# Transformer blocks on one core: the order of SyncE's queue in the block loop, the place of two turned halves, of small buffers and of the last signs

## The chip, the core and the metric

The kernel runs on one core of a Trainium2 chip. Its engines are TensorE (PE, with PEld for its weight loads), VectorE (DVE), ScalarE (ACT), GpSimd (POOL) and SyncE (SP), which here issues DMAs only. Each runs its own stream of instructions, and they order one another by semaphores that the program writes out by hand. The metric is the device time in microseconds. Three runs of the kernel before gave 2302.49, 2304.49 and 2305.18 us.

## The reference

```python
# x: 64 samples x 64 rows x 512; two layers, each x = x + ffn(cond(x))
def _L0_cond_ref(x, subjects, weights):
    return jnp.einsum('bct,bcd->bdt', x, weights[subjects])
def _L0_ffn_ref(x, w_gate_up, w_proj):
    gu = jnp.einsum('bsd,hd->bsh', x, ternary_quant(w_gate_up))
    gate, up = jnp.split(gu, 2, axis=-1)
    h = jax.nn.silu(gate) * up
    return jnp.einsum('bsh,dh->bsd', rms_norm(h), ternary_quant(w_proj))
def _L1_cond_ref(x, W, A, Bm, scalings, adapter_idx):
    H = jnp.einsum('btd,od->bto', x, W)
    xa = jnp.einsum('btd,brd->btr', x, A[adapter_idx])
    delta = jnp.einsum('btr,bor->bto', xa, Bm[adapter_idx])
    return H + delta * scalings[adapter_idx][:, None, None]
def _L1_ffn_ref(hidden_states, router_w, router_b, expert_w, expert_b):
    logits = (h @ router_w.T + router_b).reshape(T, O, E)      # O = 512, E = 8
    w, sel = jax.lax.top_k(jax.nn.softmax(logits, axis=-1), 2)
    w = w / jnp.sum(w, axis=-1, keepdims=True)
    c = jnp.zeros((T, E)).at[t_idx, sel].add(w)                # summed over O
    expert_out = jnp.einsum('th,eoh->teo', h, expert_w) + expert_b[None, :, :]
    return jnp.einsum('te,teo->to', c, expert_out)
```

## The kernel before

The 4096 rows are worked on in two big parts. The **first part** goes by blocks of 512 rows, 8 of them (`NBLK`), numbered 0 to 7. For each block PE mixes the rows with the sample's own 64x64 matrix (`mix`), then runs over 16 chunks of the hidden width (`gu`: 16 matmuls of gate and up; `proj`: 8 matmuls of the down projection of the chunk before), each value kept as a high and a low part, so that two or three matmuls make one product. In between, PE works on the block before: `adapt` (the low-rank product, behind chunk 11), `linear` (behind chunks 12 and 14). Blocks 0 and 1 are interleaved with the quantisation of the weights; blocks 2 to 6 are a hardware loop, and block 7 is written out.

For `adapt` and `linear` the second layer's input must stand with its features on the partitions. The block's result x1 is stored to DRAM by ScalarE (`store_x1`, behind chunk 0 of the next block), and SP fetches it back in 16 transfers in an order by lanes of 32 (`rows_for_turning`, line 505, transfer at line 511) into `rows_by_lane`. DVE turns it in squares of 32 (`turned`, lines 1276 to 1285) in two halves: two transposes into `cols`, ScalarE's high copy `x1t_hi` (line 832), and DVE's low part `x1t_lo` (line 1284). The first half waits for all 16 transfers (line 1279). The halves stand in DVE's stream and in ScalarE's between the chunks, so what a half waits for, the products, low parts (`hid_lo`, line 1232) and sums of the chunks behind it wait for too.

In each of four trips of SP's loop (`with sp.Fori(4, NBLK) as i`, line 519; trip i runs while block i-1 is computed, that is blocks 3 to 6) SP works off this list in order: it waits until block i-1 is mixed; loads `x_mix` for block i (1 MB); gathers eight 64x64 matrices into `mixw`; then makes the differences of the router's weights, seven times over: load a piece (line 529), wait for GpSimd's subtraction (`differences`, lines 704 to 708; line 708 is the subtraction), store it (line 531), wait for the store; and last the rows for turning of block i-2. GpSimd also makes the inverse root of the block's mean square (`power`, line 702), ahead of the differences in its stream. Block 2 has no differences: SP issues its loads and rows ahead of the loop (lines 513 to 518).

The **second part** goes by tiles of 128 rows, 32 of them (`NT`). The router stage fills 7 banks per tile, ScalarE copies them out, makes signs of them (`sign`, `place`) and DVE finds the two largest of eight (`tournament`), joins the placed signs into codes (`join`) and, between tiles, decodes codes and sums choices of earlier tiles (`decode`, `total`). The expert stage then fills 8 banks per tile: ScalarE seeds a bank with the bias (`seed_expert`, line 1098) once DVE has added the same bank of the tile before (`expert`, line 1557), and PE adds 12 matmuls to it (lines 1824 to 1828). At the change from one stage to the other, the last tile's tournament (`last_router`) lies among the experts of tile 1 on DVE; its signs and places lie on ScalarE behind seed 4 of the pass over tile 1, ahead of seeds 5 to 7, which are those of tile 2's banks; and its join stands ahead of tile 2 on DVE. SP stores the joined codes and only then goes on with the loads for tile 4 and 5. ScalarE's weights of tile 4 (`weigh`, lines 1037 and 1038) follow behind the pass over tile 1.

The buffers in SBUF are laid out by the order of the calls of `sb`: a stack that is closed gives its bytes to what is allocated next, and the program's semaphores keep the users apart.

Of the kernel before, what the change touches and what calls it, by code (L numbers as in the profile page):

```python
# [20 lines left out]
F32 = mybir.dt.float32  # L21
F32R = mybir.dt.float32r
BF16 = mybir.dt.bfloat16
I32 = mybir.dt.int32
# [5 lines left out]
P = 128  # L30
D = 512
DC = D // P
NB_SAMPLES = 64
# [9 lines left out]
E = 8  # L43
# [121 lines left out]
def build(nc, x, idx7, idx6, cond_w, w_ffn, WcT, AT, Bt, scal, rwT, rb, ewT, eb, out):  # L165
# [8 lines left out]
    with root:  # L174
        def sb(name, shape, dt, ctx=root):
            return ctx.enter_context(nc.sbuf_tensor(name, shape, dt))
# [6 lines left out]


        ident = sb("ident", [P, P], F32)


        pa = ExitStack()
# [16 lines left out]
        cols = sb("cols", [P, 2, BLK], F32, turning)  # L205
        turning.close()
        hid1 = sb("hid1", [P, RING, BLK], F32, pa)
        group_mean = sb("group_mean", [P, P], BF16, pa)
        py = ExitStack()
        y1_hi = sb("y1_hi", [P, DC, BLK], F32R, py)  # L210
        y1_lo = sb("y1_lo", [P, DC, BLK], F32R, py)
# [11 lines left out]
        x_res = sb("x_res", [P, SUB, D], F32, pa)  # L223
        sq = sb("sq", [P, BLK], F32, pa)
        sumsq = sb("sumsq", [P, BLK], F32, pa)
        ones_col = sb("ones_col", [P, 1], F32, pa)
        var = sb("var", [P, SUB], F32, pa)
        inv = sb("inv", [P, SUB], F32, pa)
        minus_half = sb("minus_half", [P, SUB], F32, pa)
        subject_i = sb("subject_i", [1, NB_SAMPLES], I32, pa)  # L230
        idx_i = sb("idx_i", [P, NB_SAMPLES], I32, pa)
        adapter_i = sb("adapter_i", [P, 1], I32, pa)
        adapter_f = sb("adapter_f", [P, 1], F32, pa)
        scal_sb = sb("scal_sb", [P, 1], F32, pa)
        lmask = sb("lmask", [P, NB_SAMPLES], F32, pa)

        pq = ExitStack()
        q_raw = sb("q_raw", [P, 3, UW], F32, pq)
# [34 lines left out]
        p4.close()  # L273
        bias_sb = sb("bias_sb", [P, E, D], F32, p2)
        wts = sb("wts", [P, 2, 2, D], F32, p2)
        step_col = sb("step_col", [P, 4], F32, p2)

        lead_in = sb("lead_in", [P, 2, D], F32, p2)
        code_in = sb("code_in", [P, 2, 2, D], BF16, p2)
        half_in = sb("half_in", [P, 4, D], U16, p2)  # L280
        digits = sb("digits", [P, 2, D], F32, p2)
        c_ring = sb("c_ring", [P, 4, E], F32, p2)
        p3 = ExitStack()
        acc = sb("acc", [P, 2, D], F32, p3)
        xin = sb("xin", [P, 2, D], F32, p3)
# [148 lines left out]
        def one(ap, i):  # L434

            if isinstance(i, int):
                return ap[i]
            names = " ".join("abcdef"[:len(ap.shape) - 1])
            return ap[bass.ds(i, 1)].rearrange(f"z {names} -> (z a) {names[2:]}"
                                               .replace("(z a)", "(z a)"))  # L440
# [3 lines left out]
        def _(sp):  # L444
            def gather_mix(i, w, done, samples=range(SPB)):
                for q in samples:
                    v = sp.value_load(subject_i[0:1, bass.ds(i * SPB + q, 1)], min_val=0, max_val=E - 1)
                    r = (q % 2) * C
                    sp.dma_start(w[r:r + C, q // 2, r:r + C],
                                 cond_w[bass.ds(v * C, C), :]).then_inc(done, 16)  # L450
# [54 lines left out]
            def rows_for_turning(l):  # L505

                sp.wait_ge(x1_stored, 16 * (l + 1) if isinstance(l, int) else sp.snap(l * 16 + 16))
                src = one(X1L, l) if isinstance(l, int) else X1L[bass.ds(l, 1)].rearrange("z a p c b j -> (z a) p c b j")
                for a in range(P // TOK):
                    for c in range(DC):  # L510
                        sp.dma_start(rows_by_lane[a * TOK:(a + 1) * TOK, c, :, :], src[a, :, c]).then_inc(rows_back, 16)  # L511
# [7 lines left out]
            with sp.Fori(4, NBLK) as i:  # L519

                mixed = sp.snap(use(i - 1, "mix1")[0] + 1)
                sp.wait_ge(drained, mixed)
                sp.dma_start(x_mix[:, :, :], one(XB, i)).then_inc(xmix_in, 16)
                gather_mix(i, mixw, mixw_in)
                piece = one(RWC, i - 4)
                sp.dma_start(diff_base[:, :], piece[0]).then_inc(diff_in, 16)
                to = one(DFC, i - 4)
                for e in range(EP):
                    sp.dma_start(diff_work[:, :], piece[e + 1]).then_inc(diff_in, 16)
                    sp.wait_ge(diff_done, sp.snap(i * EP + (e + 1 - 4 * EP)))  # L530
                    sp.dma_start(to[e], diff_work[:, :]).then_inc(diff_out, 16)
                    sp.wait_ge(diff_out, sp.snap(i * (16 * EP) + 16 * (e + 1 - 4 * EP)))
                sp.wait_ge(x1t_ready, sp.snap(i * 2 - 6))
                rows_for_turning(i - 2)


            def send_h(l, u):
# [185 lines left out]
        def _(act):  # L723
# [204 lines left out]
            def block(i):  # L928
                mix(i)
                for j in range(HC):  # L930
                    silu(i, j)
                    if j == 0:
                        store_x1(i - 1)
                    hidden(i, j)
                    if j == 2:
                        next_rows(i - 1)
                    if j in (9, 10):
                        turned(i - 1, j - 9)
                    if j == 11:
                        adapt(i - 1)  # L940
                    if j == 12 and not isinstance(i, int):
                        store_h(i - 1, 0)
                    if j == HC - 1 and isinstance(i, int):
                        copy_h(i - 1, 0)
                    if j == 14 and not isinstance(i, int):
                        store_h(i - 1, 1)
# [155 lines left out]
            def pair(m):  # L1102

                for u in range(2):
                    if not isinstance(m, int):
                        weigh(m * 2 + (u + 2), u, m + 1)
                    for e in range(E):
                        seed_expert(m * 2 + u, e)
                        if isinstance(m, int) and u == 1 and e == 4:
                            sign(NT - 1, 1, L[:, 0, EP - 1, :], (NT + 1) * KT)  # L1110
                            place(NT - 1)
                    store(m * 2 + u, u)
                    load_h(m * 2 + (u + 2), u)
# [11 lines left out]
        def _(dve):  # L1125
# [229 lines left out]
            def block(i):  # L1355
                mix(i)
                finish(i - 1)
                for j in range(HC):
                    hidden(i, j)
                    if j in (9, 10):  # L1360
                        turned(i - 1, j - 9)
                    if j == 11:
                        adapt(i - 1)
                    if j == (HC - 1 if isinstance(i, int) else 12):
                        split_h(i - 1, 0)
                    if j == 14 and not isinstance(i, int):
                        split_h(i - 1, 1)
# [190 lines left out]
                                               c_ring[:, k, e:e + 1], (xin if e == 0 else acc)[:, u, :],  # L1558
                                               ALU.mult, ALU.add).then_inc(exp_step, 1)

            def tile(n, k, pair):


                for e in range(E):
                    expert(n, e, k, pair)
                    if not isinstance(n, int) or n + 2 < NT:
                        if e == 0:
                            decode(n + 2, (k + 2) % 4)
                        total(n + 2, e, (k + 2) % 4)
# [9 lines left out]
            for e in range(E):  # L1579
                expert(1, e, 1, 0)  # L1580
                if e == 2:
                    last_router()
            join(NT - 1)
            for n in range(2, 4):
                tile(n, n, n // 2)
            with dve.Fori(1, NT // 4 - 1) as m:
                for k in range(4):
                    tile(m * 4 + k, k, m * 2 + k // 2)
# [300 lines left out]
```

## Time and profile before

| | us |
|---|---|
| median of 3 runs | 2304.49 (2302.49 to 2305.18) |
| the profiled execution | 2306.22 |
| its span | 2304.5 |
| PE busy | 2207.9 |
| DVE busy | 1625.1 |
| ScalarE busy | 1053.1 |
| GpSimd busy | 59.3 |

The span is the time from the first to the last instruction of the profiled execution. A busy time counts the engine's own instructions, not waits and not the issue of DMAs. Times of rows below are microseconds from the span's start. On the span lie the quantisation with blocks 0 and 1 (to 231), blocks 2 to 7 (block 2 from 231.06 to 340.19, blocks 3 to 6 to 858.27), the router stage (to about 1600) and the expert stage.

### The profile page before, as it was taken

To read this page: it belongs to the slowest core of one execution; us is meant where nothing else is said; L and a number is where in the kernel's file an instruction comes from. 1 tells how busy PE (TensorE), PEld (TensorE's weight loads), DVE (VectorE), ACT (ScalarE), POOL (GpSimd) and SP (SyncE) were. 2 spreads that over 40 slices of the span, in tenths; PEclk is the share of its full clock that TensorE was granted. 3 is DMA by queue.
4 is the path that set the end of the run, shared out by engine and by line. 5 is a ranking of instruction groups with operands and counts; after the bars stand their busy time and mean duration, and the time that the engine had idled before them with its cause. 6 is when DMAs were issued, how large, how long until landed. Compare 5 with 4: busy or idle time off the path is not lost.

```text
span 2304.5 us, 28740 instructions
## 1 busy us (share of the span) xinstructions
PE 2207.9 (96%) x9817; PEld 1814.9 (79%) x9817; DVE 1625.1 (71%) x2119; ACT 1053.1 (46%) x1493; POOL 59.3 (3%) x55
## 2 busy tenths in 40 slices
PE   7999999696969889999999999999999999999999
PEld 5777888585858678788888888888788888888887
DVE  8985444343433234568999999999898888888883
ACT  7754333232322223367877878778332222222221
POOL 0000001010010100200000000000000000000000
PEclk9999999898989989999999999999999999999999
DMA  6314213231322312532121212116322222222220
GB/s 206 106 41 140 76 37 116 46 116 46 116 64 76 100 40 55 187 110 87 69 77 68 82 68 82 68 68 241 110 96 82 77 96 82 78 96 77 83 82 23
DMA packets 157908, 205.66 MB, mean 89 GB/s; under 512 B 63330, under 2 KB 96674, under 8 KB 155682
## 3 DMA queue, kind: packets, MB, share of 16 engines
q1 hardware_dynamic: 114578, 149.95, 19.6%
q10 hardware_dynamic: 43152, 55.06, 7.3%
q8 instruction: 22, 0.36, 0.1%
q14 instruction: 28, 0.23, 0.0%
q0 software_dynamic: 128, 0.07, 0.0%
HBM read 136.35 MB, written 68.68 MB: 89 GB/s over the span
## 4 chain that ended last, share of the span: by engine, by line
PE 76%; issue 14%; DVE 3%; POOL 2%; ACT 1%; SPq 1%; DMA 1%; POOLq 0%; ACTq 0%; DVEq 0%
PE slot L1650 10%; PE ex_bank L1825 9%; PE ex_bank L1827 9%; PE ex_bank L1826 9%; PE high_bank L1792 5%; PE high_bank L1794 5%; PE high_bank L1796 5%; PE pj L1663 5%; PE low_bank L1792 4%; PE low_bank L1796 4%; PE low_bank L1794 4%; PE slot L1712 3%; POOL diff_work L708 2%; PE slot L1619 1%; SPq L511 1%
## 5 line engine op out<-in xcount | busy, mean ns | idle before, releaser
L1650 PE MATMUL slot<-y_hi,wgu 128*128 128x512 f32 x1024 | 402.0, 393 | 1.1 <-DVE q_scale L1168 0.5
L1650 PE MATMUL slot<-y_lo,wgu 128*128 128x512 f32 x1024 | 399.4, 390 | 0.0
L1825 PE MATMUL ex_bank<-ew_hi,hb 128*128 128x512 f32 x992 | 387.3, 390 | 3.5 <-ACT ex_bank L1098 3.5
L1826 PE MATMUL ex_bank<-ew_hi,hb 128*128 128x512 f32 x992 | 386.8, 390 | 0.0
L1827 PE MATMUL ex_bank<-ew_lo,hb 128*128 128x512 f32 x992 | 386.8, 390 | 0.0
L1098 ACT ACTIVATE ex_bank<-eb_sb 128x512 f32<-128x512 f32 x248 | 149.1, 602 | 456.5 <-DVE acc L1557 395.4
L1507 DVE SCALAR_TENSOR_TENSOR lead_in<-code_in,wts 128x1024 bf16<-128x1024 bf16 x256 | 311.8, 1218 | 1.8 <-DVE code_in L1434 0.4
L1663 PE MATMUL pj<-wpj,hid_hi 128*128 128x512 f32 x484 | 194.7, 402 | 72.5 <-DVE hid_lo L1232 72.5
L1650 PEld LDWEIGHTS slot<-y_hi,wgu 128*128 128x128 f32 x1024 | 192.3, 188 | 44.6 <-DVE q_scale L1168 2.8
L1650 PEld LDWEIGHTS slot<-y_lo,wgu 128*128 128x128 f32 x1024 | 192.4, 188 | 39.7
L1825 PEld LDWEIGHTS ex_bank<-ew_hi,hb 128*128 128x128 f32 x992 | 186.7, 188 | 42.6 <-ACT ex_bank L1098 3.9
L1826 PEld LDWEIGHTS ex_bank<-ew_hi,hb 128*128 128x128 f32 x992 | 186.7, 188 | 38.6
L1827 PEld LDWEIGHTS ex_bank<-ew_lo,hb 128*128 128x128 f32 x992 | 186.6, 188 | 38.8
L1210 DVE TENSOR_TENSOR hid<-gate,slot 128x512 f32<-128x512 f32 x112 | 76.9, 687 | 198.7 <-ACT gate L778 197.9
L778 ACT ACTIVATE gate<-slot 128x512 f32<-128x512 f32 x128 | 76.3, 596 | 284.5 <-PE slot L1650 245.4
L1792 PE MATMUL high_bank<-rw_hi,hb 128*128 128x512 f32 x512 | 199.5, 390 | 0.0
L1794 PE MATMUL high_bank<-rw_hi,hb 128*128 128x512 f32 x512 | 199.4, 390 | 0.0
L1796 PE MATMUL high_bank<-rw_lo,hb 128*128 128x512 f32 x512 | 199.4, 389 | 0.0
L1663 PE MATMUL pj<-wpj,hid_lo 128*128 128x512 f32 x484 | 192.5, 398 | 0.0
L1557 DVE SCALAR_TENSOR_TENSOR acc<-ex_bank,c_ring,acc 128x512 f32<-128x512 f32 x193 | 144.6, 749 | 67.9 <-PE ex_bank L1827 64.8
L1663 PEld LDWEIGHTS pj<-wpj,hid_hi 128*128 128x128 f32 x484 | 93.0, 192 | 93.8 <-DVE hid_lo L1232 74.2
L1792 PE MATMUL low_bank<-rw_hi,hb 128*128 128x512 f32 x384 | 149.6, 390 | 0.0
(169 smaller groups left out, 3560.6 us busy)
## 6 DMA issues: line engine op xcount, KB each, us to landing
hb<-h_scratch SPq DMA_DIRECT2D x34, 512.0 KB, 3.5
code_scratch<-half_code SPq DMA_DIRECT2D x32, 512.0 KB, 2.6
half_in<-code_scratch SPq DMA_DIRECT2D x32, 512.0 KB, 3.3
hb<-h_scratch ACTq DMA_DIRECT2D x30, 512.0 KB, 3.6
h_scratch<-ht ACTq DMA_DIRECT2D x48, 256.0 KB, 2.9
q_raw<-in_w_ffn SPq DMA_DIRECT2D x21, 512.0 KB, 3.4
x_scratch<-x_res ACTq DMA_DIRECT2D x8, 1024.0 KB, 4.4
lead_scratch<-lead SPq DMA_DIRECT2D x32, 256.0 KB, 2.0
```

The lines of the kernel that those rows point to most:

```text
L1098: nc.scalar.activation(ex[e][:, :], eb_sb[:, e, :], ACT.Copy).then_inc(ex_seeded, 1)
L1210: nc.vector.tensor_tensor(hid[:, j % 2, :], gate[:, g, :], slot[s % 2][:, 1, :], ALU.mult).then_inc(drained, 1)
L1507: nc.vector.scalar_tensor_tensor(lead_in[:, k % 2, :].bitcast(BF16).rearrange("p (a n) -> p a n", a=2), code_in[:, k % 2, :, :], float(2 * ...
L1557: nc.vector.scalar_tensor_tensor((res if e == E - 1 and not first else acc)[:, u, :], ex[e][:, :], c_ring[:, k, e:e + 1], (xin if e == 0 e ...
L1650: last = mm(slot[s % 2][:, g, :], wgu[:, c, r * P:(r + 1) * P], y[:, c, :], start=(c == 0 and v == 0), stop=(c == DC - 1 and v == 1))
L1663: last = mm(pj[k][:, :], h[:, k * P:(k + 1) * P], wpj[:, w, :], start=(j == 0 and v == 0), stop=(j == HC - 1 and v == 1))
L1792: mm(plane[k][:, :], hb[:, u, c, 0, :], rw_hi[:, k, c, :], start=False, stop=False, skip_group_check=True)
L1794: mm(plane[k][:, :], hb[:, u, c, 1, :], rw_hi[:, k, c, :], start=False, stop=False, skip_group_check=True)
L1796: last = mm(plane[k][:, :], hb[:, u, c, 0, :], rw_lo[:, k, c, :], start=False, stop=True, skip_group_check=True)
L1825: mm(ex[e][:, :], hb[:, u, c, 0, :], ew_hi[:, e, c, :], start=False, stop=False, skip_group_check=True)
L1826: mm(ex[e][:, :], hb[:, u, c, 1, :], ew_hi[:, e, c, :], start=False, stop=False, skip_group_check=True)
L1827: last = mm(ex[e][:, :], hb[:, u, c, 0, :], ew_lo[:, e, c, :], start=False, stop=(c == DC - 1), skip_group_check=True)
```

## The change

Five edits:

- In SP's loop the rows for turning, with their two waits, go ahead of the differences, and the load of `x_mix` goes behind them, to the end of the trip.
- The two turned halves go one chunk forward, behind chunks 8 and 9 instead of 9 and 10, on ScalarE and on DVE.
- Thirteen small buffers are allocated at the front of SBUF, behind `ident`; everything else shifts.
- ScalarE's last sign and place go behind the last seed of that pass (`e == EP`, seven) instead of behind the fifth.
- DVE's last join goes from in front of tile 2 to behind its expert 4.

```diff
@@ -183,6 +183,24 @@
         ident = sb("ident", [P, P], F32)
+        early_small = ExitStack()
+        group_mean = sb("group_mean", [P, P], BF16, early_small)
+        ones_col = sb("ones_col", [P, 1], F32, early_small)
...
+        scal_sb = sb("scal_sb", [P, 1], F32, early_small)
+        lmask = sb("lmask", [P, NB_SAMPLES], F32, early_small)
+        early_small.close()
+        late_small = ExitStack()
+        step_col = sb("step_col", [P, 4], F32, late_small)
+        c_ring = sb("c_ring", [P, 4, E], F32, late_small)
+        late_small.close()
+        small_end = sb("small_end", [P, 320], F32)
...
@@ -520,8 +525,9 @@
                 mixed = sp.snap(use(i - 1, "mix1")[0] + 1)
                 sp.wait_ge(drained, mixed)
-                sp.dma_start(x_mix[:, :, :], one(XB, i)).then_inc(xmix_in, 16)
                 gather_mix(i, mixw, mixw_in)
+                sp.wait_ge(x1t_ready, sp.snap(i * 2 - 6))
+                rows_for_turning(i - 2)
                 piece = one(RWC, i - 4)
                 sp.dma_start(diff_base[:, :], piece[0]).then_inc(diff_in, 16)
                 to = one(DFC, i - 4)
@@ -530,8 +536,7 @@
                     sp.wait_ge(diff_done, sp.snap(i * EP + (e + 1 - 4 * EP)))
                     sp.dma_start(to[e], diff_work[:, :]).then_inc(diff_out, 16)
                     sp.wait_ge(diff_out, sp.snap(i * (16 * EP) + 16 * (e + 1 - 4 * EP)))
-                sp.wait_ge(x1t_ready, sp.snap(i * 2 - 6))
-                rows_for_turning(i - 2)
+                sp.dma_start(x_mix[:, :, :], one(XB, i)).then_inc(xmix_in, 16)
@@ -934,8 +939,8 @@
-                    if j in (9, 10):
-                        turned(i - 1, j - 9)
+                    if j in (8, 9):
+                        turned(i - 1, j - 8)
@@ -1106,7 +1111,7 @@
                         seed_expert(m * 2 + u, e)
-                        if isinstance(m, int) and u == 1 and e == 4:
+                        if isinstance(m, int) and u == 1 and e == EP:
                             sign(NT - 1, 1, L[:, 0, EP - 1, :], (NT + 1) * KT)
                             place(NT - 1)
@@ -1357,8 +1362,8 @@
-                    if j in (9, 10):
-                        turned(i - 1, j - 9)
+                    if j in (8, 9):
+                        turned(i - 1, j - 8)
@@ -1558,11 +1563,13 @@
-            def tile(n, k, pair):
+            def tile(n, k, pair, between=None):
                 for e in range(E):
                     expert(n, e, k, pair)
+                    if e == 4 and between is not None:
+                        between()
@@ -1580,9 +1587,8 @@
-            join(NT - 1)
-            for n in range(2, 4):
-                tile(n, n, n // 2)
+            tile(2, 2, 1, lambda: join(NT - 1))
+            tile(3, 3, 1)
```

## Rows read from the trace of the kernel before

**Rows 1.** The page, part 1: busy us, share of span, instructions.

```profile
PE 2207.9 (96%) x9817; PEld 1814.9 (79%) x9817; DVE 1625.1 (71%) x2119; ACT 1053.1 (46%) x1493; POOL 59.3 (3%) x55
```

**Rows 2.** Windows, PE alone: stretch, length, busy (matmuls), granted clock, DMA share, GB/s.

```profile
231.06:340.19 109.13, 108.70 (x499) 1.00 0.20 55
340.19:858.27 518.08, 444.06 (x1987) 0.92 0.27 80
```

**Rows 3.** Waits of PE: whom it waited for, us in total, times, longest.

```profile
PE pj L1663 <- DVE hid_lo L1232: 72.5, 4, 19.3
...
PE ex_bank L1825 <- ACT ex_bank L1098: 3.5, 1, 3.5
```

**Rows 4.** Timeline, DVE, block 4: start, us, line, operation [idle before <- releaser].

```profile
507.85 1.50 DVE L1232 TENSOR_TENSOR hid_lo<-hid,hid_hi 128x512 fp32r<-128x512 f32 x1 [0.70 <-ACT hid_hi L789]
...
549.66 1.30 DVE L1281 STREAM_TRANSPOSE cols<-rows_by_lane 128x512 f32<-128x512 f32 x2 [18.76 <-DMA rows_by_lane<-x_scratch]
```

**Rows 5.** Timeline, SP's DMA queue, block 3.

```profile
346.26 0.42 SPq L523 DMA_DIRECT2D x_mix<-in_x  x1
347.55 10.53 SPq L449 DMA_DIRECT2D mixw<-in_cond_w  x8
358.26 0.44 SPq L526 DMA_DIRECT2D diff_base<-in_rwT  x1
...
411.54 8.29 SPq L511 DMA_DIRECT2D rows_by_lane<-x_scratch  x16
```

**Rows 6.** Timeline, SP's DMA queue, block 2.

```profile
238.15 10.47 SPq L449 DMA_DIRECT2D mixw<-in_cond_w  x8
248.74 12.05 SPq L511 DMA_DIRECT2D rows_by_lane<-x_scratch  x16
```

**Rows 7.** Chain that ended last, block 2: start, us, what.

```profile
279.12 3.63 PE slot L1650 x16
282.75 1.81 PE pj L1663 x8
...
301.31 3.06 PE slot L1701 x12
```

**Rows 8.** Timeline, DVE, block 2.

```profile
291.46 1.30 DVE L1281 STREAM_TRANSPOSE cols<-rows_by_lane 128x512 f32<-128x512 f32 x2
...
296.40 0.69 DVE L1232 TENSOR_TENSOR hid_lo<-hid,hid_hi 128x512 fp32r<-128x512 f32 x1 [0.70 <-ACT hid_hi L789]
...
300.04 1.22 DVE L1284 TENSOR_TENSOR x1t_lo<-cols,x1t_hi 128x1024 fp32r<-128x1024 f32 x1 [1.13 <-ACT x1t_hi L832]
```

**Rows 9.** Windows, PE alone, behind the gap of block 4.

```profile
555.00:560.00 5.00, 4.26 (x9) 0.50 0.00 0
```

**Rows 10.** Source line 523, the load of x_mix in the loop.

```profile
DMA to landing us min/median/max: 5.3/5.4/5.5
```

**Rows 11.** Timeline, GpSimd, block 4.

```profile
507.50 1.30 POOL L708 TENSOR_TENSOR diff_work<-diff_work,diff_base 128x512 f32<-128x512 f32 x1 [5.76 <-DMA diff_work<-in_rwT]
```

**Rows 12.** Timeline, ScalarE, change from router to experts.

```profile
1651.59 0.61 ACT L1015 ACTIVATE sgn<-L 128x512 bf16<-128x512 f32 x1
...
1659.54 1.62 ACT L1098 ACTIVATE ex_bank<-eb_sb 128x512 f32<-128x512 f32 x3
1661.10 0.61 ACT L1037 ACTIVATE wts<-lead_in 128x512 f32<-128x512 f32 x1
```

**Rows 13.** Timeline, DVE, same stretch.

```profile
1659.67 1.22 DVE L1415 TENSOR_TENSOR half_code<-sgn 128x2048 uint16<-128x2048 uint16 x1 [6.30 <-ACT sgn L1024]
```

**Rows 14.** Timeline, PE, same stretch.

```profile
1656.33 0.39 PE L1827 MATMUL ex_bank<-ew_lo,hb 128*128 128x512 f32 x1
...
1664.50 0.40 PE L1825 MATMUL ex_bank<-ew_hi,hb 128*128 128x512 f32 x1
```

**Rows 15.** Windows: length, then busy us (instructions) of PE, PEld, DVE, ACT, POOL.

```profile
1200.00:1400.00 200.00, 200.00 (x884) 165.68 (x883) 197.03 (x196) 162.03 (x212) 0.00 (x0) 1.00 0.21 76
...
1700.00:2290.00 590.00, 590.00 (x2605) 488.79 (x2604) 474.57 (x760) 158.07 (x265) 0.00 (x0) 1.00 0.24 80
```

More of the change, by code:

```diff
@@ L185, in build @@
         ident = sb("ident", [P, P], F32)
+        early_small = ExitStack()
+        group_mean = sb("group_mean", [P, P], BF16, early_small)
+        ones_col = sb("ones_col", [P, 1], F32, early_small)
+        var = sb("var", [P, SUB], F32, early_small)
+        inv = sb("inv", [P, SUB], F32, early_small)
+        minus_half = sb("minus_half", [P, SUB], F32, early_small)
+        subject_i = sb("subject_i", [1, NB_SAMPLES], I32, early_small)
+        idx_i = sb("idx_i", [P, NB_SAMPLES], I32, early_small)
+        adapter_i = sb("adapter_i", [P, 1], I32, early_small)
+        adapter_f = sb("adapter_f", [P, 1], F32, early_small)
+        scal_sb = sb("scal_sb", [P, 1], F32, early_small)
[6 more added lines that the diff above has]
+        small_end = sb("small_end", [P, 320], F32)
         pa = ExitStack()
@@ L207, in build @@
         hid1 = sb("hid1", [P, RING, BLK], F32, pa)
-        group_mean = sb("group_mean", [P, P], BF16, pa)
         py = ExitStack()
@@ L225, in build @@
         sumsq = sb("sumsq", [P, BLK], F32, pa)
[L226 to L235, printed above, removed]
         pq = ExitStack()
@@ L275, in build @@
         wts = sb("wts", [P, 2, 2, D], F32, p2)
-        step_col = sb("step_col", [P, 4], F32, p2)
         lead_in = sb("lead_in", [P, 2, D], F32, p2)
@@ L281, in build @@
         digits = sb("digits", [P, 2, D], F32, p2)
-        c_ring = sb("c_ring", [P, 4, E], F32, p2)
         p3 = ExitStack()
```

## The prediction

> **What bounds the kernel now.** I read the page first: TensorE is busy for 2207.9 us of a span of 2304.5 us, so at most some 97 us can be won without taking matmuls away [rows 1]. The reader is to ask where PE stands still. The stretches by block answer it: block 2 of the first phase lasts 109.13 us with PE busy for 108.70, while blocks 3 to 6 together last 518.08 us, 129.5 each, with PE busy for 444.06 and a mean granted clock of 0.92 [rows 2]. So four blocks of the same work are 20 us longer than the one before them. The wait list names the gap: PE's largest wait is at the down projection, 72.5 us in 4 waits, for a hid_lo of DVE; a single one of 3.5 us, for a seeded expert bank, matters below [rows 3]. DVE's own rows then tell why hid_lo is late: it sat 18.76 us in front of the first turn of a block, waiting for the DMA into rows_by_lane [rows 4]. In SyncE's queue, in block 3, stand the load of x_mix at 346.26, eight gathers from 347.55, the weight differences from 358.26, and only at 411.54 the sixteen transfers of the rows [rows 5]. In block 2, where no differences are made, the rows go out at 248.74, 17.7 us into the block, right behind the gathers [rows 6]. The bound of blocks 3 to 6 is therefore the order of SP's queue; in all else PE bounds.
>
> **Rows ahead of the differences.** Positions in a block are counted from its first mix matmul (231.06, 340.19, [rows 2]). SP now starts at about +6.1 with the gathers (346.26 - 340.19); they end at +16.6, x_mix's issue of 1.3 us being gone from their front [rows 5]. The rows follow. Two waits stand before them: one for the turned rows of two blocks earlier, long met, and one for the stored x1. In block 2 neither held SP up: gathers and rows follow each other without a gap [rows 6]. Price of the sixteen issues: 8.29 us when alone [rows 5], 12.05 us in block 2, where they lie beside ScalarE's load of x_res [rows 6]. That is the new situation, so I take 12.05, and the rows are issued by +28.6. DVE wants them behind chunk 8. In block 2 it began to turn behind chunk 9 at 291.46, +60.4 [rows 8]; a chunk is 3.63 + 1.81 = 5.44 us of PE [rows 7], so the new moment is +55.0. The rows have 26 us in hand, and DVE's wait goes wholly.
>
> The Trainium skill ("DMA: Bandwidth & Descriptors", Issuing engines are not separate DMA queues) speaks against the move: DMAs of SP and ScalarE run on the same 16 DMA engines and interleave. The trace agrees, 12.05 against 8.29 us; either value leaves the sum as it is.
>
> What is late next? With no wait left, PE itself. Block 2 had one more, 109.13 - 108.70 = 0.43 us, and it is the wait for x1t_lo: DVE's x1t_lo ran from 300.04 to 301.26 and PE's adapter product started at 301.31 [rows 7, 8]. Turning a chunk earlier puts x1t_lo at about 295.8 and PE needs it at 300.9, so these 0.43 us go too. A block then costs 108.70. Blocks 3 to 6: 518.08 - 4 x 108.70 = **83.3 us**. Of these 74.0 are idle PE (518.08 - 444.06) and 9.3 are slow matmuls (444.06 - 434.8): behind the gap the granted clock stands at 0.50, that is 1.2 GHz, and is at 2.4 again after it [rows 9]. Both go with the gap. Blocks 2 and 7 had no gap and give back 0.43 each: **0.9 us**.
>
> **What the move pushes back.** Behind the rows on SP stand the differences, which GpSimd waits for, and then the load of x_mix, which the next block's first matmul waits for. The differences took 411.54 - 358.26 = 53.3 us [rows 5]; they now run from +28.6 to +81.9. GpSimd is free again before the next block's power wants it, behind +108.7, so that costs nothing. x_mix is issued at +81.9, lands within 5.5 us [rows 10], at +87.7, and is wanted at +108.7: 21 us of cover. Each microsecond beyond them would cost one in each of four blocks. SP itself is free again before the next block's mark, so the delay doesn't pile up.
>
> **Turning behind chunks 8 and 9.** The same transposes, copies and subtractions, one chunk earlier, each still ahead of the next product. DVE's low part for chunk 10 ended in block 2 at 296.40 + 0.69 = 297.1 [rows 8], where it stood behind one turned half, as it will now; proj(10) wants it at 299.1 (adapter product 300.9 less 1.81). So about 2 us are in hand, 1 to 2 with the small shifts that I can't read. What could eat them is GpSimd: a subtraction of differences at 507.50 lies across DVE's 507.85, and that took 1.50 us instead of 0.69 [rows 4, 11]. Differences come once in some 7 us and now fall into the turning window. One hit of up to 1.3 us mostly fits into the slack; I charge 0.1 us for each of four blocks, **-0.4 us**, with 0 and -5.2 (a full 1.3 each) as ends.
>
> The Trainium skill ("SBUF — State Buffer", SBUF: two separate sides) has the rule: GpSimd and a DVE operation with two SBUF inputs hold a shared port pair exclusively, and the loser blocks for the whole instruction. This trace agrees (the 1.50 us); the result of the rule here is the rival of hits below.
>
> **Small buffers first.** Addresses move, no instruction is added. Every wait in this kernel is a semaphore written by hand, so no order changes. The trace can't show whether a new address makes an operation quicker or slower; I take zero, the nearest thing being that nothing in the argument so far rests on an address, and keep a rival for it. Most exposed would be DVE in the router stage, busy for 197.03 of 200 us [rows 15].
>
> **Last signs behind the third tile's seeds.** Today ScalarE makes the last sign at 1651.59 and the places, and only then the three seeds, at 1659.54 [rows 12]. PE's last matmul of the group before starts at 1656.33, and a matmul takes 5.44 / 24 = 0.227, so the next group was due at 1656.56 and the one after it, 12 matmuls on, at 1659.28; that one began at 1664.50 [rows 14]. Lost: **5.2 us**, 3.5 of them the wait [rows 3] and the rest matmuls at the low clock. With all seeds first, they are done at about 1654.0, and sign and places (8.0 us, 1651.59 to 1659.54) end at 1662.0. Behind them in ScalarE's queue stand the two weights of tile 4 (from 1661.10, some 1.1 us, [rows 12]) and the first seed for tile 3. That seed then ends near 1663.7, and PE, 5.2 us ahead, wants it at 1656.56 + 3 x 2.72 = 1664.7: 1.0 us of slack. The last join leaves DVE's path in front of tile 2, where DVE idled 6.30 us [rows 13], and goes behind tile 2's expert 4. DVE now waits for tile 4's weights instead, until 1663.1, as it starts them near that time today, and catches up: in the expert stage it is busy for 474.57 us of 590 [rows 15]. SP's store of the last codes waits for that join until about 1671.6, 11 us later than now, and behind it stand the loads for tiles 4 and 5. They would be in by some 1677 and are wanted near 1679. A miss would hold DVE, not PE, which then has more than 10 us in banks. I take the full 5.2; the bounds are 0 and 5.5.
>
> **Sum.** 83.3 + 0.9 + 5.2 - 0.4 = 89.0 us. The profiled execution took 2306.2 us, 1.7 us around its span; it becomes 2217.2. The median of the three runs is 2304.49, 1.7 lower, and 2304.49 - 89.0 = **2215.5 us**.
>
> **Rivals.**
> - *GpSimd's hits count, or a turned half delays a projection.* For it: [rows 4, 11] and the thin slack. Against it: one difference in 7 us. At one full hit a block the time is 2220, at two some 2226. Chance 0.08.
> - *The seeds' slack of 1.0 us fails or the late weights hold DVE and then PE.* Up to 5.2 us are lost: 2220.7. Chance 0.05.
> - *x_mix takes the place of the rows.* From +108.7 on, the next mix waits for it. SP would have to be 21 us later than I work out, for instance by differences that take 11 us each instead of 7.6. At 10 us beyond, 2255. Chance 0.02.
> - *It doesn't do what it says: the rows were not the last thing that DVE waited for.* Then the blocks stay near 129 us and 5 us are won, 2299. Block 2 with early rows and no gap speaks against it. Chance 0.01.
> - *Slower than before: the new addresses slow DVE in the router stage.* It has 1.5% to spare there [rows 15]. Beyond that each per cent costs about 6 us over some 600 us; from 17% on (1.5 to spare, 15 to pay back the 89) the kernel is slower than before; at 20% 2325. No row hints at it. Chance 0.01.
> - *More is won than PE's rows show*, some 2209. Chance 0.03.
>
> The forecast with its own range of 2212 to 2219 has the remaining 0.80. To hold 8 in 10 with the unknown slacks, I reach to the first two rivals: **2210 to 2224**. About 0.2% (4.6 us) is what a measurement of this kernel can tell from no change. Faster by more: 0.98; within: 0.01; slower: 0.01.
>
> **What the changed profile would show.** Blocks 3 to 6 at 108.7 us each with a granted clock of 1.00; no PE wait for hid_lo; no DVE wait for rows_by_lane; rows issued near +17 and x_mix near +82 on SP; PE's wait for x1t_lo gone; no wait of 3.5 us at the expert banks, ScalarE's sign near 1654 less 84. Wrong would be: mix waiting for x_mix, stretched DVE subtractions next to a PE wait at the projection, or PE waiting for a seed of tile 3.

## The result and the profile after

Four runs of the changed kernel gave 2212.77 to 2214.39 us, median **2213.6 us**, beside 2304.02 us (2302.49 to 2305.18) of the kernel before: a ratio of 0.961, with an interval of 0.959 to 0.963. The profiled execution took 2214.39 us. Its page, span, part 1 and the shares of the chain that ended last:

```profile
span 2212.7 us, 28732 instructions
...
PE 2192.0 (99%) x9809; PEld 1809.1 (82%) x9817; DVE 1627.9 (74%) x2119; ACT 1053.4 (48%) x1493; POOL 60.3 (3%) x55
...
PE 93%; issue 4%; DVE 2%; ACT 1%; POOL 1%; ACTq 0%; POOLq 0%; DVEq 0%
```

PE is busy for all but 20.7 us of the span, against 96.6 before [rows 1]. Windows of PE alone by block, blocks 2 to 6 of the changed kernel (stretch, length, busy with matmuls, granted clock, DMA share, GB/s):

```profile
231.16:339.06 107.90, 107.90 (x498) 1.00 0.21 56
339.06:446.96 107.90, 107.90 (x498) 1.00 0.32 96
446.96:556.17 109.21, 108.21 (x498) 1.00 0.32 95
556.17:665.37 109.20, 108.20 (x498) 1.00 0.32 95
665.37:773.27 107.90, 107.90 (x498) 1.00 0.32 96
```

The 518.08 us of blocks 3 to 6 [rows 2] are now 434.21, and the granted clock is 1.00 in every block. Two things were not foreseen: a block can be shorter than 108.70 us, and two of the four are 1.3 us longer than the others. The waits of PE say what the two have (engine, line, releaser: us in total, times, longest):

```profile
PE slot L1635 <- ACT q_mag L753: 8.2, 3, 5.4
PE pj L1669 <- DVE hid_lo L1237: 2.0, 2, 1.0
```

The first stands in the quantisation, ahead of the block loop. The second is the wait of [rows 3], with 2.0 us in two waits where there were 72.5 in four. SP's queue in block 3, which starts at 339.06:

```profile
345.81 10.33 SPq L454 DMA_DIRECT2D mixw<-in_cond_w  x8
356.50 12.13 SPq L516 DMA_DIRECT2D rows_by_lane<-x_scratch  x16
368.83 0.36 SPq L532 DMA_DIRECT2D diff_base<-in_rwT  x1
...
418.56 0.38 SPq L539 DMA_DIRECT2D x_mix<-in_x  x1
```

Against [rows 5]: the rows now go out at +17.4 in the block instead of +71.4, and take 12.13 us beside the other loads, as in [rows 6]; x_mix goes out at +79.5, 28.4 us before the next block's first matmul (446.96 - 418.56). PE shows no wait for it.

At the change from router to experts, first ScalarE, then DVE (start, us, line, operation [idle before <- releaser]):

```profile
1566.84 0.60 ACT L1103 ACTIVATE ex_bank<-eb_sb 128x512 f32<-128x512 f32 x1 [0.18 <-DVE res L1562]
1567.38 0.62 ACT L1020 ACTIVATE sgn<-L 128x512 bf16<-128x512 f32 x1
...
1576.38 0.58 ACT L1103 ACTIVATE ex_bank<-eb_sb 128x512 f32<-128x512 f32 x1
```

```profile
1576.51 1.23 DVE L1512 SCALAR_TENSOR_TENSOR lead_in<-code_in,wts 128x1024 bf16<-128x1024 bf16 x1 [5.81 <-ACT wts L1043]
...
1583.74 1.22 DVE L1420 TENSOR_TENSOR half_code<-sgn 128x2048 uint16<-128x2048 uint16 x1
```

The seeds of tile 2 end at 1567.4 with the sign behind them, where before they waited for it [rows 12]; PE's wait of 3.5 us is gone. DVE still idles 5.81 us, as before 6.30 [rows 13], but for tile 4's weights, and the join comes later: counted from block 7's adapter product on PE (976.18 before, 890.08 after), at 693.7 instead of 683.5 us.

### The profile page after: what moved, and what is told of

Its sections match the earlier page's. It is cut to its first block, busy times and chain, and to the rows that moved or that the text cites. A ratio compares the mean times of both kernels' runs of the same rounds, so it can differ in the third digit from the quotient of the medians.

```text
span 2212.7 us, 28732 instructions
## 1 busy us (share of the span) xinstructions
PE 2192.0 (99%) x9809; PEld 1809.1 (82%) x9817; DVE 1627.9 (74%) x2119; ACT 1053.4 (48%) x1493; POOL 60.3 (3%) x55
## 4 chain that ended last, share of the span: by engine, by line
PE 93%; issue 4%; DVE 2%; ACT 1%; POOL 1%; ACTq 0%; POOLq 0%; DVEq 0%
PE slot L1656 18%; PE ex_bank L1833 10%; PE ex_bank L1831 10%; PE ex_bank L1832 10%; PE pj L1669 9%; PE high_bank L1800 5%; PE high_bank L1798 5%; PE high_bank L1802 5%; PE low_bank L1800 4%; PE low_bank L1798 4%; PE low_bank L1802 4%; PE slot L1718 3%; PE slot L1625 1%; PE slot L1707 1%; PE ex_bank L1846 1%
## 5 line engine op out<-in xcount | busy, mean ns | idle before, releaser
L1798 PE MATMUL low_bank<-rw_hi,hb 128*128 128x512 f32 x384 | 149.4, 389 | 0.0
L1800 PE MATMUL low_bank<-rw_hi,hb 128*128 128x512 f32 x384 | 149.4, 389 | 0.0
```

Of the source, the lines that this page charges most:

```text
L1798: mm(plane[k][:, :], hb[:, u, c, 0, :], rw_hi[:, k, c, :], start=False, stop=False, skip_group_check=True)
L1800: mm(plane[k][:, :], hb[:, u, c, 1, :], rw_hi[:, k, c, :], start=False, stop=False, skip_group_check=True)
```

## The experiments

Each kernel ran beside the kernel before, whose median was 2303.41 us in the first group of runs, 2302.96 in the second and 2304.63 in the third. Times are medians.

### The parts of the change, one at a time

**Small buffers alone** (layout_only): the kernel before with the third edit.

```diff
+        early_small = ExitStack()
+        group_mean = sb("group_mean", [P, P], BF16, early_small)
...
+        small_end = sb("small_end", [P, 320], F32)
```

> The kernel before with the small buffers at the front and nothing else. In the trace of before, matmuls whose moving operand is x1t or xa (adapter and linear products, 72 per block, 576 in all) start every 0.2333 us, all others every 0.2267; in the changed kernel all start every 0.2267, and x1t begins 32 bytes further on, at a multiple of 64 instead of 32 bytes beside one. Address theory: these 576 matmuls win 0.0066 us each, 3.8 us, and some 50 of the quantisation 0.3 more: about 2300.0, with the four gaps unchanged. Rival (my prediction's zero: the slower spacing comes from the waits of the old order, not from the address): 2304.0, spacing still 0.2333.

Measured: 2299.76 us, ratio 0.998 (0.997 to 0.999), 3.7 us less than before (the interval goes from 2.1 to 6.0). The step of the prediction that took zero for it falls. The lines view of PE by form (busy, mean ns | idle before) shows the place, first before, then layout_only:

```profile
L1712 PE MATMUL slot<-x1t_hi,wc_hi 128*128 128x512 f32 x128 | 50.8, 397 | 0.0
```

```profile
L1717 PE MATMUL slot<-x1t_hi,wc_hi 128*128 128x512 f32 x128 | 49.9, 390 | 0.0
```

Its gaps in blocks 3 to 6 stayed, 72.7 us in 4 waits.

**SP's order alone** (sp_only): the kernel before with the first edit.

```diff
-                sp.dma_start(x_mix[:, :, :], one(XB, i)).then_inc(xmix_in, 16)
                 gather_mix(i, mixw, mixw_in)
+                sp.wait_ge(x1t_ready, sp.snap(i * 2 - 6))
+                rows_for_turning(i - 2)
...
-                sp.wait_ge(x1t_ready, sp.snap(i * 2 - 6))
-                rows_for_turning(i - 2)
+                sp.dma_start(x_mix[:, :, :], one(XB, i)).then_inc(xmix_in, 16)
```

> The kernel before with SP's queue reordered and nothing else. Theory: the gap in blocks 3 to 6 goes wholly, each block then lasts what block 2 lasted before, 109.1 us, so 518.1 - 436.5 = 81.6 us are won: 2222.4, and PE keeps its wait of 0.4 us for x1t_lo in each block. If GpSimd's subtractions hit the turning, up to 1.3 us per block more: 2222 to 2227. Rival (the turned halves' place is part of the cure): clearly more than 2227.

Measured: 2227.69 us, ratio 0.967 (0.965 to 0.968), 75.7 us less than before, just above the range. No wait for hid_lo is left; PE's waits have instead

```profile
PE slot L1701 <- DVE x1t_lo L1284: 5.4, 6, 1.4
```

So the gap is the order of SP's queue. With the halves still behind chunks 9 and 10, nothing lies between the second half and the adapter product, and what delays DVE reaches PE there. GpSimd does so too: in block 3 a subtraction at 409.18 stands ahead of the second half's x1t_lo at 409.49, which takes 2.07 us instead of 1.23.

**Turning earlier alone** (turn_only): the kernel before with the second edit.

```diff
-                    if j in (9, 10):
-                        turned(i - 1, j - 9)
+                    if j in (8, 9):
+                        turned(i - 1, j - 8)
```

> The kernel before with the turned halves behind chunks 8 and 9 and nothing else. Theory: the rows still come behind the differences at the same moment, but DVE now stands still one chunk earlier, so one more chunk of 5.44 us of PE lies behind the gap in each of four blocks, +21.8, less the small waits for x1t_lo (0.4 to 0.7 in six blocks): about 2322. Rival (a chunk earlier is a gain by itself, or nothing): 2301 to 2304.

Measured: 2322.07 us, ratio 1.008 (1.006 to 1.009). DVE in block 3:

```profile
421.06 1.30 DVE L1281 STREAM_TRANSPOSE cols<-rows_by_lane 128x512 f32<-128x512 f32 x2 [25.84 <-DMA rows_by_lane<-x_scratch]
```

The rows come when they came; DVE gets in line for them one chunk earlier, and one more chunk is stuck behind it. The wait of PE grew from 72.5 to 92.5 us.

**The late turn in the changed kernel** (late_turn): all edits but the second.

```diff
-                    if j in (8, 9):
-                        turned(i - 1, j - 8)
+                    if j in (9, 10):
+                        turned(i - 1, j - 9)
```

> The changed kernel with the turned halves back behind chunks 9 and 10. Theory: PE waits for x1t_lo again before the adapter product, 0.43 us and some 0.3 of matmuls that start slowly behind it, in six blocks, and as no chunk lies between the second half and the adapter, each microsecond that a subtraction on GpSimd takes from DVE goes to PE: 0.7 x 6 + about 2.8 - the 2.6 that the hits cost now: 2216 to 2219. Rival (the turned halves' place is worth nothing once the rows are early): 2213 to 2214.

Measured: 2217.36 us, 3.8 us above the changed kernel, with 4.0 us of waits for x1t_lo (6 times, 0.8 at most). So turning a chunk earlier costs 18.7 us alone and gains 3.8 beside early rows.

**Last signs alone** (signs_only): the kernel before with the fourth and fifth edits.

```diff
-                        if isinstance(m, int) and u == 1 and e == 4:
+                        if isinstance(m, int) and u == 1 and e == EP:
...
-            join(NT - 1)
...
+            tile(2, 2, 1, lambda: join(NT - 1))
```

> The kernel before with the last sign, place and join moved and nothing else. Theory: the wait of 3.5 us and the slow matmuls behind it go, 5.2 to 5.7 us: about 2298.6, no PE wait for a seed. Rival (ScalarE's place and weights then delay tile 3's seed, or DVE's wait for the weights holds PE): 2300 to 2304, with a PE wait for a seed in tile 3.

Measured: 2298.52 us, ratio 0.998 (0.997 to 0.999), 4.9 us less than before (2.5 to 6.4), and no wait for ex_bank.

### What the addresses do

**The turned halves 32 bytes on** (x1t_off32): in the changed kernel, x1t_hi and what follows it move away from the weights.

```diff
+        off = sb("off", [P, 8], F32, pa)
         x1t_hi = sb("x1t_hi", [P, DC, BLK], F32R, pa)
```

> The changed kernel with 32 unused bytes ahead of x1t, so that x1t, xa and the buffers behind them begin 32 bytes beside a multiple of 64 again, and nothing else. Address theory: the 576 matmuls that move x1t or xa start every 0.2333 us again, 3.8 us slower: 2217.4. Rival (another effect of the layout): 2213.6 and spacing 0.2267.

Measured: 2218.59 us, 5.0 above the changed kernel. The slow matmuls are back:

```profile
L1719 PE MATMUL slot<-x1t_hi,wc_hi 128*128 128x512 f32 x128 | 50.7, 396 | 0.0
```

PE waits for hid_lo in three blocks here, not in two, which is 1.3 of the 5.0; the other 3.7 are the addresses (576 x 0.0066 us = 3.8).

**Everything 32 bytes on** (all_off32): the spacer behind the small buffers grows, and all later buffers move together.

```diff
-        small_end = sb("small_end", [P, 320], F32)
+        small_end = sb("small_end", [P, 328], F32)
```

> The changed kernel with the reserved space at the front 32 bytes longer, so that every buffer behind it begins 32 bytes beside a multiple of 64. Address theory: every 512-column matmul with a float32 moving operand starts 0.0066 us later than it could; some 9500 of them are on the path, so about 60 us: 2270 to 2280; more if the weights' address counts too. Rival (the slower spacing is peculiar to x1t's place): at most 4 us, 2217.

Measured: 2214.95 us, 1.3 above the changed kernel and with the third wait for hid_lo as well, so no cost of the addresses is left. The first of these matmuls' three kinds:

```profile
L1718 PE MATMUL slot<-x1t_hi,wc_hi 128*128 128x512 f32 x128 | 49.9, 390 | 0.0
```

My theory in its first form, that the moving operand's own address decides, falls: at 32 beside a multiple of 64 the matmuls were fast. What remains is the difference of the two operands. In these matmuls the weights are the stationary operand and the turned half is the moving one. The table has the remainders mod 64 of their addresses, and the mean time of the first kind of linear's matmuls. The traces print no addresses; the remainders are added up from the sizes of the buffers in the order of the calls of `sb`.

| kernel | weights wc | turned x1t | mean ns |
|---|---|---|---|
| before | 0 | 32 | 397 |
| layout_only | 0 | 0 | 390 |
| after | 0 | 0 | 390 |
| x1t_off32 | 0 | 32 | 396 |
| all_off32 | 32 | 32 | 390 |

**The same for the router and the experts** (hb_off32b): hb, the stationary operand of both stages, lies 32 bytes beside a multiple of 64, and the moving weights at a multiple. All of the first part's buffers move by 32 together, so that their operands stay equal.

```diff
+        off_a = sb("off_a", [P, 8], F32, pa)
         wgu = sb("wgu", [P, DC, 2 * HID], F32R, pa)
...
+        off = sb("off", [P, 8], F32, pbc)
         hb = sb("hb", [P, 2, DC, 2, P], F32R, pbc)
```

> The changed kernel with 32 unused bytes ahead of hb (the stationary operand of the router and expert stages) and 32 ahead of all buffers of the first part. So hb begins 32 bytes beside a multiple of 64 while the router's and experts' weights, the moving operands, begin at a multiple; in the first part both operands lie 32 beside. Seen so far: 0.2333 us a matmul where x1t lay 32 bytes beside and its weights did not, 0.2267 where neither or both did. Theory (what counts is that the two operands differ modulo 64): the 5800 matmuls of the two stages cost 0.0066 us more each, 38 us: about 2252, the first part unchanged. Rival (only a moving operand that lies beside costs, or x1t's place is peculiar): 2213 to 2218.

Measured: 2252.91 us, ratio 0.977 (0.976 to 0.979), 39.3 above the changed kernel. First the changed kernel, then this one:

```profile
L1831 PE MATMUL ex_bank<-ew_hi,hb 128*128 128x512 f32 x992 | 385.9, 389 | 0.0
```

```profile
L1833 PE MATMUL ex_bank<-ew_hi,hb 128*128 128x512 f32 x992 | 392.3, 396 | 0.0
```

Some 5800 matmuls have hb as stationary operand, and 5800 x 0.0066 us = 38 us; a third wait for hid_lo, as in x1t_off32, makes up the other 1.3. In the first part, where both operands now lie at 32, linear's matmuls stay at 390 ns. So the difference of addresses is shown at two places and in both directions: with x1t the moving operand was the one at 32, with hb the stationary one. Why the hardware minds is not shown.

### GpSimd's subtractions

Block 2, which starts at 231.16, has no differences. There DVE makes chunk 10's low part, behind both turned halves:

```profile
297.21 0.69 DVE L1237 TENSOR_TENSOR hid_lo<-hid,hid_hi 128x512 fp32r<-128x512 f32 x1 [0.70 <-ACT hid_hi L794]
```

Timelines of the changed kernel in block 4, which starts at 446.96: GpSimd's subtraction, and DVE.

```profile
500.93 1.61 POOL L713 TENSOR_TENSOR diff_work<-diff_work,diff_base 128x512 f32<-128x512 f32 x1 [5.58 <-DMA diff_work<-in_rwT]
```

```profile
500.70 0.69 DVE L1237 TENSOR_TENSOR hid_lo<-hid,hid_hi 128x512 fp32r<-128x512 f32 x1 [0.70 <-ACT hid_hi L794]
501.31 1.78 DVE L1248 TENSOR_TENSOR sumsq<-sumsq,sq 128x512 f32<-128x512 f32 x1
```

And in block 3, which starts at 339.06:

```profile
393.81 1.44 POOL L713 TENSOR_TENSOR diff_work<-diff_work,diff_base 128x512 f32<-128x512 f32 x1 [5.62 <-DMA diff_work<-in_rwT]
```

```profile
393.41 0.69 DVE L1248 TENSOR_TENSOR sumsq<-sumsq,sq 128x512 f32<-128x512 f32 x1
```

DVE's sum begins at +54.35 in both. GpSimd begins at +53.97 in block 4 and the sum takes 1.78 us; at +54.75 in block 3 and it takes 0.69. The sum stands right ahead of the turned half, and what it loses goes to the low part of chunk 10. The second hit of block 4 is the sum at 508.56 (1.79 us); a third, at 515.82, lies behind both halves. The subtraction of the second hit, and the low part ahead of it:

```profile
508.36 1.44 POOL L713 TENSOR_TENSOR diff_work<-diff_work,diff_base 128x512 f32<-128x512 f32 x1 [5.82 <-DMA diff_work<-in_rwT]
```

```profile
507.96 0.69 DVE L1237 TENSOR_TENSOR hid_lo<-hid,hid_hi 128x512 fp32r<-128x512 f32 x1 [0.70 <-ACT hid_hi L794]
```

**Almost no subtraction** (diffs_tiny): GpSimd subtracts 8 of 512 columns; the rest of the weight differences is left out.

```diff
-                    nc.gpsimd.tensor_tensor(diff_work[:, :], diff_work[:, :], diff_base[:, :], ALU.subtract).then_inc(diff_done, 1)
+                    nc.gpsimd.tensor_tensor(diff_work[:, 0:8], diff_work[:, 0:8], diff_base[:, 0:8], ALU.subtract).then_inc(diff_done, 1)
```

> The changed kernel with GpSimd subtracting 8 columns of 512, so most of the router weights' differences are left out; the loads, stores and waits stay. In the changed kernel two DVE sums of blocks 4 and 5 take 1.78 us instead of 0.69 and PE waits 1.0 us for hid_lo in each of these blocks. Theory (GpSimd's subtraction shuts DVE out): no DVE operation is stretched, both waits go, blocks 4 and 5 last 107.9 like 3 and 6: 2.6 us won, 2211.0. Rival (DVE is late for another reason, for instance the DMAs of the differences): 2213.6, sums still stretched.

Measured: 2211.73 us, 1.9 less than the changed kernel, where 2.6 were expected; the medians of the kernel before in the four groups of runs differ by 1.7 us, so the verdict rests on the trace: no wait for hid_lo is left. The sums by source line in blocks 2 to 7 (ns least/median/most), first the changed kernel, then this one:

```profile
L1248 DVE TENSOR_TENSOR sumsq<-sumsq,sq x76: 678/686/1786, 247.4 to 789.5; 128x512 f32<-128x512 f32 x76
```

```profile
L1248 DVE TENSOR_TENSOR sumsq<-sumsq,sq x76: 683/686/689, 246.0 to 785.5; 128x512 f32<-128x512 f32 x76
```

**A chunk between the halves** (turned_7_9): in the changed kernel the halves go behind chunks 7 and 9, so that DVE can catch up in between.

```diff
-                    if j in (8, 9):
-                        turned(i - 1, j - 8)
+                    if j in (7, 9):
+                        turned(i - 1, (j - 7) // 2)
```

> The changed kernel with the turned halves behind chunks 7 and 9 instead of 8 and 9. Theory: DVE works off its backlog of 0.7 us in the chunk between them, so the product of chunk 10 starts some 0.7 us earlier and two subtractions of GpSimd fit into the slack; PE's waits for hid_lo go, the rows have landed 18 us before they are wanted: 2211.0. Rival (the waits depend only on how GpSimd's subtractions happen to lie): 2213 to 2215.

Measured: **2210.61 us** (2210.34 to 2211.02), ratio 0.959 (0.958 to 0.961): 3.0 less than the changed kernel, with its slowest run under that kernel's fastest, and no wait for hid_lo. It is the fastest kernel of this study with the whole computation in it. Its sums in blocks 2 to 6 show 689 ns at most, so in this run no subtraction of GpSimd came ahead of one: it also moved the phase. The subtractions met low parts instead: in block 3 those at 386.21 (1.41 us) and at 393.08 (1.43 us), around the first half, and in block 6 two as well, and PE waited for none. So two hits fit here, but how much of the 3.0 us is the spare chunk and how much the phase isn't separated.

### How much cover x_mix has

**Each difference stored twice**, and **three times** (stores_twice, stores_thrice, with 3 for 2): SP's list gets longer behind the rows.

```diff
-                    sp.dma_start(to[e], diff_work[:, :]).then_inc(diff_out, 16)
-                    sp.wait_ge(diff_out, sp.snap(i * (16 * EP) + 16 * (e + 1 - 4 * EP)))
+                    for r in range(2):
+                        sp.dma_start(to[e], diff_work[:, :]).then_inc(diff_out, 16)
+                        sp.wait_ge(diff_out, sp.snap(i * (16 * EP * 2) + 16 * (e * 2 + r + 1 - 4 * EP * 2)))
```

> The changed kernel with each of the seven differences stored twice, one store after the other, each waited for (2.5 us more each). That puts x_mix's load 17.5 us later, to about 97.0 us into the block, landing near 102.4, ahead of the mix at 107.9. Theory (some 21 to 23 us of cover): no wait at the mix, 2213.6, give or take 2.6 for GpSimd's subtractions lying otherwise. Rival (x_mix or the power behind the differences is already close to the bound): 10 us or more slower.

> The same with three stores of each difference, 35 us more: x_mix lands near 119.9 us into the block. Theory: PE waits 12 us for it at the first matmul of blocks 4 to 7, 48 us in all, and the matmuls behind each wait run at the low clock for about 2.3 us' worth, as behind the gaps of before: 2213.6 + 48 + 9 = 2271. Rival (SP's delay is carried over from block to block and grows): clearly more, over 2290; or (no cost at all): 2214.

Measured: 2211.81 us with two stores; x_mix goes out at 436.65, +97.1 in the block, 17.6 us later than in the changed kernel (+79.5), and nobody waits for it. Its hid_lo waits are gone too; the differences lie elsewhere against the chunks, one in some 9.5 us. With three, 2272.86 us, ratio 0.986 (0.984 to 0.987), and PE's largest wait is

```profile
PE slot L1626 <- DMA x_mix<-in_x: 49.6, 4, 12.9
```

The chain that ended last, at the start of block 4 (start, us, what):

```profile
454.62 5.21 DMA x_mix<-in_x
459.82 0.22 issue
460.04 6.67 PE slot L1626 x32
```

The 32 mix matmuls take 6.67 us behind the wait, and 3.57 us at full clock (559.74 - 556.17 = 3.57 in the changed kernel's chain). So a block pays its 12.4 us of wait and about 3 us behind it: (2272.86 - 2211.81) / 4 = 15.3.

## Why the prediction held, step by step

Forecast were 2215.5 us with a range of 2210 to 2224, measured 2213.6. The mechanism held; three sizes in it were off, and they partly cancel.

- **The bound of blocks 3 to 6 is SP's order.** Shown: sp_only takes the gap away, and the edits that leave the order alone keep it. Predicted 83.3 - 0.4 = 82.9 us, measured 518.08 - 434.21 = 83.9. That the slow matmuls behind the gap go with it was right too: the granted clock is 1.00.
- **The positions.** Gathers to +17.1, the rows issued in 12.13 us (12.05 taken), x_mix at +79.5 (+81.9 foreseen). The cover foreseen was 21 us, and is 28.4 - 5.4 = 23.0. An issue 17.6 us later in the block cost nothing (stores_twice, block 3 starting at 339.52), and one 35.6 us later (stores_thrice, 454.47 in a block starting at 339.32) should cost 12.6 and cost 12.4 in the mean, 12.9 at most.
- **Block costs 108.70.** Mis-sized. A block without a hit takes 107.90. One term that was wrong is **small buffers at zero**: linear's 60 matmuls of a block have a turned half or the low-rank product xa as moving operand, and 60 x 0.0066 = 0.40 us. Of the rest of the 0.80, 0.34 lies at the adapter product, whose 12 matmuls took 3.06 us right behind a short wait [rows 7] and take 2.72 without one; in layout_only and late_turn they took 3.06 behind that wait with equal addresses as well. The prediction gave back the wait of 0.43 us and not this. In the trace the first number was to be seen before: linear's matmuls at 397 ns beside 390 ns for the same size elsewhere. The argument rested on sums of PE alone.
- **Hits of GpSimd.** Mis-sized. Charged 0.4 us in all; two of four blocks lost 1.3 each, 2.6. That is the sign of being wrong that the prediction names, stretched work of DVE next to a PE wait at the projection. Two steps behind the charge were off. The first is the slack of about 2 us: it lets chunk 10's low part stand behind one turned half, as in [rows 8], but with the halves behind chunks 8 and 9 it stands behind both, and DVE comes to it 0.7 us later. In block 2 of the changed kernel it begins at 297.21 and ends at 297.90, and its projection starts at 299.16, so 1.3 us are in hand. One hit does fit into that, as the prediction has it: in block 3 a subtraction stretched a low part to 1.38 us (387.36), and PE didn't wait. The second is the number of hits. Unhit, the sums ahead of the two halves stand 6.15 us apart (block 3); a hit makes it 7.25, and the subtractions stand 7.43 apart, so where the first of these sums is hit, the second is too: 2 x 1.1 - 1.3 = 0.9 us, and PE waits for 1.0, with 0.3 more in the matmuls behind the wait (2.12 instead of 1.81 us). Diffs_tiny shows the cause.
- **Blocks 2 and 7.** 0.9 us foreseen; 109.13 - 107.90 = 1.2 and some 1.1 measured, by the addresses and the adapter product.
- **Hand-off.** 5.2 us foreseen; about 5.7 measured, from block 7's adapter product to the end (1328.3 us before, 1322.6 after). The 0.5 over the forecast are addresses again: block 7's 72 matmuls of adapt and linear lie in this stretch, and from their first to the router's next matmul it is 16.81 us before and 16.35 after. In signs_only, where no address moved, the same stretch to the end takes 1323.0 us (from 973.09), 5.3 less than before; its median gave 4.9. Moved by the 86.10 us that block 7's adapter product came earlier, the sign at 1567.38 stands at 1653.5 (1654.0 foreseen), tile 3's seed ends at 1663.1 (1663.7), and DVE's wait for tile 4's weights ends at 1662.6 (1663.1); PE has no wait there.
- **Sum.** 83.9 + 1.2 + 1.1 + 5.7 = 91.9 by spans (2304.5 - 2212.7 = 91.8), against 89.0. The 2.9 more are some 2.9 of addresses (6 x 0.40 and block 7's 0.46) and 2.0 at the adapter product (6 x 0.34), against 2.2 more of hits, 2.7 in all. The wrong terms had opposite signs, so the forecast was nearer than its parts deserved: that is luck. By medians the parts alone give 75.7 + 3.7 + 4.9 us and the early turn beside early rows 3.8, 88.1 of 90.4; the rest isn't placed.
- **Rivals.** "More is won than PE's rows show" and "hits count" both came true in part. x_mix in place of the rows is real, but starts some 20 us further on (stores_thrice). That new addresses could slow DVE in the router stage is not borne out; the addresses act on PE instead, and there the wrong offset for hb would have taken 39 of the 91 us. Turning earlier without early rows is the way in which one of these edits really is slower than before: 2322 us.

## What to carry to other kernels

When one queue carries work of different urgency, look in it for what an in-order engine waits for, and put that first; measure then how far the thing pushed back can slide, as the store test did here. An edit that is good only beside another one should be tried both ways: turning earlier lost 18.7 us alone and won 3.8 with the rows early. Compare the mean time of equal instructions across lines before calling a move of buffers free.

## What was not expected of the hardware

**Matmul spacing.** Matmuls of 512 columns start every 0.2333 us (396 ns each) when the addresses of the stationary and the moving operand differ by 32 bytes mod 64, and every 0.2267 us (389 ns) when they are equal, at 0 or at 32. Only differences of 0 and 32 bytes were tried. The Trainium skill ("SBUF — State Buffer", Operand start alignment) treats the start of an operand as a question of what is allowed and says that its runs timed nothing; the time is new here.

**Who begins first.** A sum of DVE takes 1.78 us instead of 0.69 if GpSimd's subtraction began 0.38 us ahead of it, and its usual time if GpSimd began 0.40 us behind it. The Trainium skill ("SBUF — State Buffer", SBUF: two separate sides) says that whichever starts first holds the port pair for its whole instruction and the other waits. The trace agrees, for GpSimd's own time too. The subtraction took 1.30 us where no low part or sum of DVE was running when it began [rows 11], although it stretched the low part behind it [rows 4]. It took 1.61 us at 500.93, 0.23 us into the low part of 500.70, and 1.44 us at 508.36, 0.40 us into the low part of 507.96. Both add up to the same: 0.23 + 0.31 and 0.40 + 0.14, so GpSimd got going 0.54 us after the low part's start, and then stood ahead of the sum. So the 0.3 us are GpSimd's wait for the low part, and not a price of being first. Since nothing ties the differences to the chunks, 0.8 us of phase decide on 1.3 us of a block. Splitting the differences around the turning, which would tie them, was not tried.
